# Gated FFN after cross-attention scores: new orders around the first gates, and the last row turned by DMA

## The reference, cut to what matters

```python
x = x + tanh(g_xattn[0]) * xattn(ctx, layernorm(x), W, b)
x = x + tanh(g_ffn[0]) * ffn(layernorm(x), w1, w2, w3)

def xattn(x, adj, W, b):             # si, sj: one score per context row
    xij = sigmoid(si[:, :, None] + sj[:, None, :] + b[0])
    return 0.6 * xij + 0.4 * adj

def bitlinear(x, w):                 # every one of the three products
    xn = x * rsqrt(mean(x * x) + 1e-6)
    xq = clip(round(xn * s), -128, 127) / s        # s = 127 / max|xn| of the row
    wq = clip(round(w * sw), -1, 1) / sw           # sw = 1 / mean|w| of the whole weight
    return xq @ wq.T

def ffn(x, w1, w2, w3):
    return bitlinear(silu(bitlinear(x, w1)) * bitlinear(x, w2), w3)
```

## Time and profile before

| | |
|---|---|
| runs (three), median | 156.69, 157.48, 157.88 us; 157.48 us |
| profiled execution, its own time | 155.58 us |
| span of the profiled execution | 153.8 us |
| PE busy | 137.7 us, 90% |
| DVE busy | 119.3 us, 78% |
| ACT busy | 106.7 us, 69% |
| POOL busy | 96.8 us, 63% |
| granted clock of PE, mean | 0.999 |

### The profile page before, as it was taken

The page is one execution under the profiler, slowest core; times in us unless marked ns, Lnnn a source line. Parts: engine busy times, 40 slices in busy tenths (PEclk is TensorE's granted clock), DMA queues, the critical chain, the costliest instruction groups (busy, mean ns, idle before and its releaser), DMA issues.

```text
span 153.8 us, 2452 instructions
## 1 busy us (share of the span) xinstructions
PE 137.7 (90%) x754; PEld 76.4 (50%) x754; DVE 119.3 (78%) x185; ACT 106.7 (69%) x174; POOL 96.8 (63%) x151
## 2 busy tenths in 40 slices
PE   0940879959999999999999999999999999999993
PEld 0830779646565454444444444445444444454562
DVE  0519899989999999899966599989499384678542
ACT  3067898999969986689878426996595745754530
POOL 3302797999993928898379407896906797098400
PEclk9999999999999999999999999999999999999999
DMA  4899999999492583786616600826363447309723
GB/s 147 276 391 395 409 398 417 400 368 371 120 133 59 106 169 75 151 146 124 162 34 125 165 4 17 213 83 149 70 169 74 157 84 175 66 0 170 184 111 136
DMA packets 45381, 26.94 MB, mean 175 GB/s; under 512 B 35767, under 2 KB 38072, under 8 KB 45368
## 3 DMA queue, kind: packets, MB, share of 16 engines
q1 hardware_dynamic: 45360, 26.78, 63.1%
q10 hardware_dynamic: 8, 0.00, 0.0%
HBM read 13.89 MB, written 4.19 MB: 118 GB/s over the span
## 4 chain that ended last, share of the span: by engine, by line
PE 67%; POOL 12%; DMA 7%; DVE 6%; issue 3%; SPq 2%; ACT 2%; ACTq 0%; DVEq 0%; POOLq 0%
PE ps L1255 42%; PE ps L1299 23%; DMA c_all<-in_x_dram 7%; POOL raw L502 2%; POOL ln_r L433 2%; POOL w3q L505 2%; PE ps L1294 2%; DVE raw_room L980 1%; SPq L287 1%; POOL xq L487 1%; POOL c_all L448 1%; ACT raw_room L704 1%; POOL slope_mean L437 1%; DVE w1T L985 1%; POOL slope L436 1%
## 5 line engine op out<-in xcount | busy, mean ns | idle before, releaser
L1255 PE MATMUL ps<-w1T,xqT 128*128 128x512 f16 (+1 forms) x192 | 40.6, 361 | 0.1
L1255 PE MATMUL ps<-w2T,xqT 128*128 128x512 f16 (+1 forms) x192 | 40.7, 361 | 0.0
L1004 DVE SCALAR_TENSOR_TENSOR raw<-ps,deq,raw_room 128x1408 f32<-128x1408 f32 x16 | 26.9, 1684 | 16.2 <-PE ps L1255 8.4
L1299 PE MATMUL ps<-w3T,hqT 128*128 128x512 f16 x165 | 37.7, 379 | 0.0
L704 ACT ACTIVATE raw_room<-ps,deq 128x1408 f32<-128x1408 f32 x16 | 22.9, 1430 | 12.3 <-PE ps L1255 12.3
L514 POOL TENSOR_SCALAR hq<-raw,h_scale 128x1408 f16<-128x1408 f32 x15 | 22.1, 1473 | 12.1 <-DVE h_scale L1014 11.7
L1255 PEld LDWEIGHTS ps<-w2T,xqT 128*128 128x128 f16 x192 | 18.7, 98 | 19.9 <-DVE raw L1004 0.6
L1255 PEld LDWEIGHTS ps<-w1T,xqT 128*128 128x128 f16 x192 | 18.6, 98 | 19.7 <-ACT raw_room L704 0.4
L715 ACT ACTIVATE junk<-raw 128x1410 f16<-128x1410 f32 x16 | 21.9, 1371 | 7.6 <-DVE raw L1004 7.6
L1011 DVE TENSOR_REDUCE h_top<-raw 128x1 f32<-128x1409 f32 x16 | 25.8, 1610 | 0.2
L1299 PEld LDWEIGHTS ps<-w3T,hqT 128*128 128x128 f16 x165 | 16.0, 98 | 18.2 <-issue 0.3
(11 more groups left out here) (102 smaller groups left out, 180.9 us busy)
## 6 DMA issues: line engine op xcount, KB each, us to landing
c_all<-in_x_dram SPq DMA_DIRECT2D x16, 256.0 KB, 9.4
out_dram<-out_ring SPq DMA_DIRECT2D x15, 256.0 KB, 2.3
raw<-in_L_ffn_w_dram SPq DMA_DIRECT2D x4, 704.0 KB, 11.2
raw_room<-in_L_ffn_w_dram SPq DMA_DIRECT2D x3, 768.0 KB, 8.7
raw<-in_L_ffn_w_dram SPq DMA_DIRECT2D x3, 768.0 KB, 11.8
hq<-in_ctx_dram SPq DMA_DIRECT2D x4, 256.0 KB, 10.2
raw_room<-in_L_ffn_w_dram SPq DMA_DIRECT2D x1, 512.0 KB, 10.8
raw<-in_L_ffn_w_dram SPq DMA_DIRECT2D x1, 512.0 KB, 10.5
```

Of the source, the lines that this page charges most:

```text
L1004: v.scalar_tensor_tensor(out=hid[:, t % HS, 0:H], in0=ps_up[:, 0:H], scalar=deq[:, 1, t:t + 1], in1=gate[:, t % GATES, :], op0=ALU.mult, o ...
L1255: last = m.matmul(bank[:, lo:hi], xqT[:, i % XT, k, :], wT[w][:, k, lo:hi], start=(k == 0), stop=(k == KD - 1))
L1299: last = m.matmul(ps_y[t % 2], hqT[:, t % HT, k, :], w3T[:, :, k, :], start=(k == 0), stop=(k == KH - 1))
```

## The change

Four things. `make_x` and `max_x` go by a finer list, `PARTS`, in which tiles 2 to 5 are alone; the other steps keep `UNITS`. `intercept` is one instruction for a unit instead of one for each tile. The queues are put in another order between the first `gate_product` and tile 5. The last hidden row is quantized in one piece and turned by DMA as all others, so that `turn_last` and both `evac_last` are gone. Below, `...` marks what is left out.

```diff
+    PARTS = [(0, 1), (1, 2), (2, 3), (3, 4), (4, 5), (5, 6)] + UNITS[4:]
+    PART = [n for n, (lo, hi) in enumerate(PARTS) for _ in range(lo, hi)]
...
             def turn_h(t):
-                sp.wait_ge(hq_done, t + 1)
+                if t == T - 1:
+                    sp.wait_ge(hq_last, 1)
+                else:
+                    sp.wait_ge(hq_done, t + 1)
...
             turn_x(4)
+            turn_h(0)
+            turn_x(5)
             turn_w3(2)
-            turn_x(5)
-            turn_h(0)
             turn_w3(3)
...
             turn_h(14)
+            turn_h(15)
             store(11)
...
@@ POOL @@
             def quant_x(i):
-                pool.wait_ge(x_scaled, UNIT[i] + 1)
+                pool.wait_ge(x_scaled, PART[i] + 1)
...
             mean_x(0)
+            quant_x(2)
             conv_w(2, 0)
-            quant_x(2)
             quant_x(3)
+            step_x(2)
+            dequant_x(2)
+            slopes_x(3)
             conv_w(2, 1)
-            slopes_x(3)
-            step_x(2)
             conv_w(2, 2)
-            dequant_x(2)
             quant_x(4)
             quant_h(0)
+            conv_w(2, 3)
+            quant_x(5)
             step_x(3)
-            quant_x(5)
+            dequant_x(3)
             mean_x(1)
-            dequant_x(3)
-            conv_w(2, 3)
             quant_x(6)
@@ ACT @@
             evac_w(1, 1)
+            ctx_out(2)
+            silu(0)
             sum_w(2, 1)
             sum_w(2, 2)
-            ctx_out(2)
-            silu(0)
             evac_w(1, 4)
+            evac_w(1, 5)
             square_x(2)
-            evac_w(1, 5)
+            silu(1)
+            square_x(3)
+            scores_out(2)
             score(4)
             score(5)
-            scores_out(2)
-            silu(1)
-            square_x(3)
             ctx_out(3)
-            score(6)
+            silu(2)
             affine_x(4)
             affine_x(5)
+            score(6)
             score(7)
-            silu(2)
+            silu(3)
             square_x(4)
             th_neg_x(1)
             score(8)
             square_x(5)
             scores_out(3)
-            silu(3)
             affine_x(6)
@@ DVE @@
             def intercept(u):
...
-                for i in range(lo, hi):
-                    ins = v.tensor_scalar(icept[:, i:i + 1], th_sum[:, i:i + 1], t03_neg[:, 0:1], slope_mean[:, i:i + 1],
-                                          ALU.mult, ALU.subtract)
-                ins.then_inc(icepts, 1)
+                v.scalar_tensor_tensor(out=icept[:, lo:hi], in0=th_sum[:, lo:hi], scalar=t03_neg[:, 0:1],
+                                       in1=slope_mean[:, lo:hi], op0=ALU.mult, op1=ALU.subtract).then_inc(icepts, 1)
...
-            def make_x(u):
-                lo, hi = UNITS[u]
+            def make_x(n):
+                lo, hi = PARTS[n]
...
             evac_w(1, 3)
-            scale_w(2)
+            half_scores(2)
             make_x(2)
             max_x(2)
-            half_scores(2)
+            make_x(3)
+            scale_w(2)
+            max_x(3)
             stats_x(3)
             stats_x(4)
+            hidden(0)
             clip_w3(0)
-            hidden(0)
-            clip_w3(1)
             intercept(3)
             max_h(0)
+            clip_w3(1)
+            make_x(4)
             half_scores(3)
-            make_x(3)
-            max_x(3)
+            max_x(4)
             hidden(1)
-            weight_factor(2)
+            make_x(5)
+            max_x(5)
             clip_w3(2)
             intercept(4)
-            max_h(1)
             hidden(2)
             clip_w3(3)
-            make_x(4)
-            max_x(4)
+            weight_factor(2)
+            max_h(1)
+            make_x(6)
+            max_x(6)
             hidden(3)
...
             max_h(15)
+            quant_last()
             add_x(11)
-            quant_last()
             add_x(12)
             add_x(13)
-            evac_last()
             finish(14)
@@ PE @@
             turn_w(1, 3)
-            sum_w(2, "x", 2)
+            scores(2, "x", 2)
             turn_w(1, 4)
-            scores(2, "sums", 3)
+            gate_product(1)
+            sum_w(2, "scores", 3)
             turn_w(1, 5)
-            gate_product(1)
             spread_scores(2)
             up_product(0)
+            gate_product(2)
             turn_ctx(3)
-            gate_product(2)
-            scores(3, "scores", 3)
             up_product(1)
+            scores(3, "sums", 3)
+            gate_product(3)
             spread_scores(3)
-            gate_product(3)
             up_product(2)
...
             last_product(13)
-            turn_last()
             last_product(14)
             last_product(15)
```

More of the change, by code:

```diff
@@ L179, in flamingo_gated_ffn @@
         ps_w16 = [ps[:, (3 + i) * BANK:(4 + i) * BANK].bitcast(F16) for i in range(3)]
-        ps_h16 = [ps[:, i * BANK:(i + 1) * BANK].bitcast(F16) for i in range(2)]
         ps_x16 = ps_y[0].bitcast(F16)[:, BANK:2 * BANK]
@@ L1117, in _ @@
             stats_x(7)
-            make_x(5)
-            max_x(5)
+            make_x(7)
+            max_x(7)
             intercept(6)
@@ L1126, in _ @@
             affine_x(11)
-            make_x(6)
+            make_x(8)
             max_h(7)
-            max_x(6)
+            max_x(8)
             add_x(3)
@@ L1135, in _ @@
             hidden(9)
-            make_x(7)
+            make_x(9)
             intercept(8)
@@ L1139, in _ @@
             affine_x(14)
-            max_x(7)
+            max_x(9)
             hidden(10)
             affine_x(15)
-            make_x(8)
+            make_x(10)
             max_h(10)
@@ L1146, in _ @@
             add_x(7)
-            max_x(8)
+            max_x(10)
             max_h(11)
@@ L1300, in last_product @@
                     last.then_inc(y_ps, 1)
-            def turn_last():
-                pe.wait_ge(silu_done, T)
-                for n, (lo, hi) in enumerate(HALVES):
-                    pe.wait_ge(hq_last, n + 1)
-                    for k in range(lo, hi):
-                        last = m.transpose(ps_h16[n][:, (k - lo) * P:(k - lo + 1) * P],
-                                           hq[:, (T - 1) % HQ, k * P:(k + 1) * P], ident16[:, :])
-                    last.then_inc(hT_ps, 1)
             pe.wait_ge(consts, 3)
```

46 lines of the change are left out of this document (12 added, 34 removed).

## The result

The changed kernel took 157.97 us in the median of 4 runs (157.73 to 159.43), the kernel before 157.08 us (154.81 to 157.88) beside it. The ratio over the comparable executions, which is not the ratio of these two medians, is 1.0216, with a 95% interval of 1.0164 to 1.0268: slower, by 1.6 to 2.7%. The forecast was no change (156.9 us, -0.4%) with a chance of 0.08 for this side; the time lies in the range of 155.9 to 158.1, the sign is wrong. The profiled execution took 157.82 us, with a span of 156.0 us, against 155.58 and 153.8.

The account below looks back on a forecast made before the run. PE was taken as the bound, never idle from 60 to 100 us, with 2.2 us of waits after the first gate product. Gates 0.0 and last row -0.6 took 157.48 to 156.9 us, range 155.9 to 158.1.

Parts of the forecast that it names:

- the 0.0 for the gates: First gates to the first last products: small waits use up the early lead, so the new order ends with 0 to 0.1 us.
- Steps 1 and 2: First gates on PE: gate_product(1) starts at 33.5, 2.4 us ahead; up_product(0) at 37.3, 1.4 us ahead, with 0.4 us idle.
- Step 3: Tile 2's transpose: issued at 37.7, landed at 40.3, so gate_product(2) starts at 40.4, 1.2 us ahead, 0.6 us idle.
- tile 2's transpose lands late: Rival, chance 0.2: tile 2 lands with the x loads at 41.0 to 41.6; 157.5 to 158.1 us.
- Step 4: DVE's row to hidden(1): split units cost 0.6 us each, fused intercept saves 0.27; up_product(2) at 49.7, 0.7 us ahead.
- Step 5: ACT's queue to silu(4): gate_product(5) starts at 57.5, where it started before; the lead is used up.
- Step 6: Scale of tiles 6 and 7 on DVE at 58.5 to 58.9, landing 64.3 to 64.8; last_product(1) had started at 64.80.
- the 1 us around 60.0: Sign: the gates forecast is wrong if PE reaches the first last_product more than 1 us sooner or later than 60.0.
- the difference is carried to the end unchanged: After last_product(1), PE has the same queue and is full, so no time is won or lost on the way.
- The last row: End of the kernel: PE loses 11 transposes, gain 0.6 us; the DMA landing is covered by 1.1 us.

Follow-up runs that it names:

- e3: Kernel before with only the last row quantized in one piece and turned by DMA; 154.62 us at full clock, ratio to before 0.9981.
- e11: Kernel before with the last row by DMA and make_x and max_x of tiles 2 to 5 single, old order, plain intercepts; 154.55 us at full clock.
- e1: Changed kernel with intercept again one plain instruction for each tile; 156.34 us at full clock, ratio to before 1.005.
- e5: Changed kernel with plain intercepts and the loads of x of tiles 10 to 15 put behind tile 3's transpose (late loads); 156.02 us at full clock.
- e9: Changed kernel, fused intercept kept, with the loads of x of tiles 10 to 15 put behind tile 3's transpose; 157.69 us at full clock.
- e2: Kernel before with only the fused intercept put in; 159.43 us in the median of 6 runs, none at full clock, ratio to before 1.0255.
- e4: Changed kernel with POOL waiting for the intercepts of units 2 and 3 before its next long instruction; 159.36 us, all at reduced clock, ratio to before 1.0246.
- e12: Changed kernel with plain intercepts, late loads of x and turn_ctx(3) back ahead of gate_product(2) on PE; 156.25 us at full clock.
- e15: Changed kernel with plain intercepts, late loads of x and the third weight's second piece converted and clipped earlier again (POOL, DVE); 156.93 us at full clock.

## Why the prediction was wrong

The term of my sum that failed is the 0.0 for the gates. It holds two terms: the new order, for which I had 0 to 0.1 us of gain, measured +2.0 us, and the fused intercept, for which I had a gain of 0.27 us each, measured +1.6.

The parts, at full clock: the last row -0.85, the split about -0.2, the new order with it +2.0, the fused form +1.6; together +2.5. (They are the steps from the kernel before over e3, e11 and e1 to the changed one, so the sum is no test; that the fused form costs 1.4 to 1.7 between e5 and e9, and 1.6 in e2 at reduced clock, is one.)

1. **Steps 1 and 2 held**: 33.45 and 37.09 (with 0.30 idle) for 33.5 and 37.3 (with 0.4).
2. **Step 3 failed.** I had tile 2's scale at 36.2, the DMA at 37.7 and its landing 2.4 to 2.6 us later. The fused intercept at 31.56 took 0.8 us more than the plain pair and shifted DVE behind it, and `quant_x(2)` on POOL took 1.11 us for the 0.69 that I had; the DMA left at 38.48. e1 shows that this was not needed to lose the lead: issued at 37.44, the transpose took 4.1 us. The rival "tile 2's transpose lands late" named this mechanism, its place (41.0 to 41.6) and its sign, and I gave it 0.2. That its 157.5 to 158.1 us hold the measured time is luck of the base again; it had a loss of 0 to 0.6 us for the 2.5 measured. What it lacked is that a landing that comes at a fixed time makes every step ahead of it worthless. The rule of the Trainium skill that I set beside it (DMA: Bandwidth & Descriptors, Queues, rings and completion order) fits the three landings at about 41.4, though no run separates it from a busy DMA.
3. **Step 4 is the term that was mis-sized.** "A fused `intercept` saves one instruction of 0.27 us" was taken as true wherever it stands. At this place it took 1.31 us instead of 0.46, a loss of 0.85 where I had a gain. e1 and e9 measure the whole at 1.4 to 1.7 us of time, of which the traces of e1 and the changed kernel account for 0.8. I had costed the instruction by its count, not by what its operands share with POOL. The rest of step 4 is late in e1 as well: `up_product(2)` at 50.71, against 51.50 in the changed kernel and 49.7 forecast.
4. **Step 5**: `gate_product(5)` at 59.14 for 57.5. In e1 it was at 58.57, behind an `ACT` bracket of 0.56 us.
5. **Step 6**: the scale of tiles 6 and 7 came at about 61.3 for 58.5 to 58.9, by this row, where the earlier trace rows had 3.53 us of waiting:

```profile
61.41 0.69 POOL L489 TENSOR_SCALAR xq<-c_all,x_scale 128x512 f16<-128x512 f32 x1 [5.18 <-DVE x_scale L938]
```

   `last_product(1)` followed at 67.22; in e1, 66.23. The chain that I drew was the right one, its two entries were late. The first `last_product`, at 61.79, is outside the 1 us around 60.0 that I had named as the sign of being wrong.
6. **From there "the difference is carried to the end unchanged"**: nearly. Another 0.36 us went ahead of 119.84, where `hidden` was late. The chain of waits leads there through `affine_x(15)`, beside an add of POOL:

```profile
113.53 1.48 DVE L915 TENSOR_SCALAR c_all<-c_all,slope,icept 128x512 f32<-128x512 f32 x1
```

```profile
113.45 1.27 POOL L534 TENSOR_TENSOR out_ring<-out_ring,c_all 128x512 f32<-128x512 f32 x1
```

   It took 0.54 us before and 0.71 in e1. The same 1.48 and the same bracket stand in e9 and e4, and in e2 1.47 with 0.56 us; no kernel with plain intercepts has the bracket. The slow intercept at 105.94 (1.23 us) is the likely reason, by way of POOL: DVE itself stood idle for 1.23 us between the two, but POOL's queue waited for the scale behind that intercept, and its add came 1.8 us later than in e1 while PE was 1.0 later, just onto `affine_x(15)`. This instruction has one tensor as input, so a plain form is no safeguard where it is wide.
7. **The last row held**: 0.6 us in the trace and 0.85 in e3.

Open: how the 2.0 us of the order share out between the landing, DVE's row to `hidden(1)` and ACT's to `silu(4)`. The late loads removed the first and returned 0.3 us; e12 and e15 changed one place each and returned nothing. None of the single places that were tried holds it.

## What to carry to other kernels

Fusing two small VectorE instructions into one with two tensors as inputs is no saving where GpSimd is in a wide instruction (here 512 columns or more): read in the trace what GpSimd runs at that time, and count the rest of that instruction as its price. Before work is moved ahead on an engine, find the event on the way that comes at its own time (here a transpose behind queued loads): what is gained ahead of it is given back there. And a bundle of edits deserves its parts one by one: here two of them alone (e11) were 1.1 us faster than before, the whole 2.5 slower.
